# Value and output projection of a shifted-window block: 64-row weights in row tiles replaced by zero-padded 128-row weights in column tiles

## The reference

```python
y = _ln(x, norm1_w, norm1_b); y = jnp.roll(y, (-3, -3), axis=(1, 2))
win = windows(y)                                   # (32 * 64, 49, 64)
q, k, v = split(win @ qkv_w.T)                     # 8 heads of 8
attn = softmax(q @ k^T * scale + bias + mask)      # 49 x 49 for each window and head
out = (attn @ v) @ proj_w.T + proj_b
x = shortcut + roll(out, (3, 3))
z = _ln(x, norm2_w, norm2_b)
return x + gelu(z @ fc1_w.T + fc1_b) @ fc2_w.T + fc2_b
```

## Time and profile before

| what | value |
|---|---|
| median of 3 runs | 2359.13 us (2358.63 to 2376.8) |
| the profiled execution, its own time | 2345.75 us |
| span of its trace | 2343.9 us |
| mean granted TensorE clock | 0.986 |
| PE busy | 2217.1 us, 95% |
| POOL, DVE, ACT busy | 76%, 75%, 66% |

### The profile page before, as it was taken

How to read it: one execution, slowest core, us unless ns; L and a number is a source line. 1 busy time by engine, 2 the same in 40 slices (tenths; PEclk the granted TensorE clock), 3 DMA queues, 4 the chain that set the end, 5 groups by cost and what they waited for, 6 DMA issues and landing times.

```text
span 2343.9 us, 155989 instructions
## 1 busy us (share of the span) xinstructions
PE 2217.1 (95%) x66852; PEld 1699.0 (72%) x66852; DVE 1756.3 (75%) x3230; ACT 1548.0 (66%) x2435; POOL 1770.1 (76%) x1687
## 2 busy tenths in 40 slices
PE   5999999999999999999999999999999999999997
PEld 4777777777777777777777777777677777777775
DVE  5787787777777877777777777777777777777774
ACT  4567666666666776766666766666666666666765
POOL 5787787777777877776777777777777777777774
PEclk7999999999999999999999999999999999999999
DMA  5444444444444454444444444444444444444541
GB/s 122 98 92 103 91 94 100 87 90 90 95 97 90 96 100 90 99 90 85 96 87 92 102 89 93 103 93 90 94 90 89 93 91 97 94 91 93 103 87 41
DMA packets 137659, 217.73 MB, mean 93 GB/s; under 512 B 29336, under 2 KB 95114, under 8 KB 137114
## 3 DMA queue, kind: packets, MB, share of 16 engines
q1 hardware_dynamic: 137114, 208.95, 43.2%
HBM read 131.69 MB, written 77.15 MB: 89 GB/s over the span
## 4 chain that ended last, share of the span: by engine, by line
PE 85%; ACT 6%; issue 5%; DMA 1%; DVE 1%; POOL 0%; SPq 0%; ACTq 0%; POOLq 0%; DVEq 0%
PE O L759 13%; PE ST L745 11%; PE S L723 9%; PE M L767 9%; PE ST L739 8%; PE M L832 7%; PE M L854 7%; PE M L818 5%; PE M L785 5%; PE M L801 5%; PE M L862 3%; ACT L456 3%; ACT gl L456 2%; PE S L727 2%; DMA xin<-in_x 0%
## 5 line engine op out<-in xcount | busy, mean ns | idle before, releaser
L337 POOL TENSOR_TENSOR nmd<-diag,nm 121x392 f16<-121x392 f16 x1024 | 897.4, 885 | 435.6 <-DVE nm L592 412.5
L592 DVE TENSOR_REDUCE nm<-S 121x8 f16<-121x392 f32 x1024 | 576.7, 563 | 375.9 <-PE S L727 185.0
L437 ACT ACTIVATE pT<-ST 113x392 f32<-113x392 f32 x1024 | 506.2, 495 | 404.7 <-PE ST L745 400.2
L759 PEld LDWEIGHTS O<-vx,pT 113*49 113x49 f32 x16384 | 552.1, 127 | 61.1 <-issue 20.5
L759 PE MATMUL O<-vx,pT 113*49 113x18 f32 x16384 | 530.7, 197 | 16.7 <-issue 14.3
L723 PE MATMUL S<-kp,qp 128*49 128x49 f16 x16384 | 395.6, 186 | 26.4 <-issue 10.7
L739 PE MATMUL ST<-qp,kp 128*49 128x49 f16 x16384 | 396.8, 186 | 23.7 <-issue 22.7
L723 PEld LDWEIGHTS S<-kp,qp 128*49 128x49 f16 x16384 | 318.3, 104 | 100.3 <-issue 75.7
L745 PE MATMUL ST<-nmd,shiftw 121*49 121x392 f16 x2048 | 362.6, 350 | 2.0 <-POOL nmd L337 1.3
L739 PEld LDWEIGHTS ST<-qp,kp 128*49 128x49 f16 x16384 | 330.1, 103 | 37.5 <-issue 27.9
L745 PEld LDWEIGHTS ST<-nmd,shiftw 121*49 121x49 f16 x2048 | 107.1, 101 | 286.4 <-issue 150.0
(11 more groups left out here) (87 smaller groups left out, 3297.6 us busy)
## 6 DMA issues: line engine op xcount, KB each, us to landing
parts<-hl SPq DMA_DIRECT2D x512, 98.0 KB, 2.6
qp<-parts SPq DMA_DIRECT2D x512, 98.0 KB
xin<-in_x SPq DMA_DIRECT2D x256, 98.0 KB
kp<-parts SPq DMA_DIRECT2D x256, 98.0 KB
kp<-parts SPq DMA_DIRECT2D x512, 49.0 KB
out<-res SPq DMA_DIRECT2D x256, 98.0 KB
kp<-in_c_keys SPq DMA_DIRECT2D x4, 588.0 KB, 8.4
weights<-in_c_weights SPq DMA_DIRECT2D x1, 384.0 KB, 3.6
```

What stands on the lines that cost most here:

```text
L337: nc.gpsimd.tensor_tensor(nmd[j % LAG][:], diag[:], nm[j % LAG][:].unsqueeze(2).broadcast_to([RM, 2 * 4, N]), ALU.mult).then_inc(s_nmd, 1)
L437: nc.scalar.activation(pT[j % LAG][:].rearrange("k w h q -> k (w h q)"), ST[0:R, j % 2, 0:HK], ACT.Exp).then_inc(s_e, 1)
L592: V.tensor_reduce(nm[j % LAG][:], S[0:RM, 0:HK].rearrange("q (h n) -> q h n", n=N), AX_X, ALU.max, negate=True).then_inc(s_nm, 1)
L759: mm = MM(O[W0 * w:W0 * w + N, (4 * p + hp) * VC:(4 * p + hp + 1) * VC], pT[j % LAG][:, w, hp, :], vx[r % RING][:, window + w, hp, :], sta ...
```

## The change

Both projections are given weights of 128 rows. A host helper `apart` makes them: the 64 x n weights stand twice, once in the upper rows with zeros in the lower ones, once in the lower rows with zeros in the upper ones, side by side in the columns. One matmul over all 128 rows then gives the results of both halves in neighbouring columns.

- `project_v`: 32 matmuls of 64 rows by 49 by 32 columns, in four tiles of the array (two row tiles by two column tiles), two banks, become 16 matmuls of 128 rows by 49 by 64 columns, in two column tiles, one bank.
- `project_out`: 8 matmuls of 64 rows by 113 by 64 columns, in two row tiles, two banks, become 8 matmuls of 128 rows by 49 by 128 columns, in two column tiles, one bank. The halves of the tokens (partitions 0 to 48, 64 to 112) are now separate matmuls.
- The readers (`place_v`, `add_attention`, and `times_v` for the places in `vx`) follow the new places. No wait is added or dropped.
- The weights' load grows from 768 to 896 columns, and DVE also clears all of `M` (128 x 2048) before it computes the tables, since rows 49 to 63 are no longer written by `project_out` and are read by `add_attention`.

```diff
             V.memset(S[:], -1.0).then_inc(c_blank, 1)
             V.memset(ST[:], 0.0).then_inc(c_blank, 1)
             V.memset(O[:], 1.0).then_inc(c_blank, 1)
+            V.memset(M[:], 0.0).then_inc(c_blank, 1)
...
-                    nc.scalar.activation(dst[rows, :, D * e:D * e + D].rearrange("n (a s) d -> n a s d", a=2),
-                                         M[rows, 2:4, 0:256].rearrange("n a (s d) -> n a s d", d=D),
+                    nc.scalar.activation(dst[rows, :, D * e:D * e + D],
+                                         M[rows, 2, :].rearrange("n (s d) -> n s d", d=D),
                                          ACT.Copy).then_inc(s_vx, 1)
...
-                V.tensor_tensor(held, M[0:R, 0:2, 0:4 * C].rearrange("r h (p c) -> r p h c", c=C), held,
+                V.tensor_tensor(held, M[0:R, 0, :].rearrange("r (p h c) -> r p h c", h=2, c=C), held,
                                 ALU.add).then_inc(s_att, 1)
...
             def project_v(u):
                 for s in range(8):
-                    for h in range(2):
-                        for e in range(2):
-                            rows = slice(C * h, C * h + C)
-                            mm = MM(M[W0 * e:W0 * e + N, 2 + h, 32 * s:32 * s + 32], yT[rows, N * s:N * s + N],
-                                    wv[rows, e, :], start=True, stop=True, tile_position=(C * h, W0 * e))
+                    for e in range(2):
+                        mm = MM(M[W0 * e:W0 * e + N, 2, C * s:C * s + C], yT[:, N * s:N * s + N], wv[:, e, :],
+                                start=True, stop=True, tile_position=(0, W0 * e))
                 mm.then_inc(s_vp, 1)
...
                 for q in range(4):
-                    for h in range(2):
-                        rows = slice(C * h, C * h + C)
-                        mm = MM(M[0:R, h, C * q:C * q + C], oT[rows, q, :], wproj[rows, :], start=True, stop=True)
+                    for w in range(2):
+                        mm = MM(M[W0 * w:W0 * w + N, 0, 2 * C * q:2 * C * q + 2 * C], oT[:, q, W0 * w:W0 * w + N], wproj,
+                                start=True, stop=True, tile_position=(0, W0 * w))
                 mm.then_inc(s_pj, 1)
...
+    def apart(a):
+        a = np.asarray(a).reshape(C, -1, a.shape[-1])
+        both = np.zeros((2, C, a.shape[1], 2, a.shape[2]), np.float32)
+        both[0, :, :, 0], both[1, :, :, 1] = a, a
+        return both.reshape(2 * C, -1)
```

More of the change, by code:

```diff
@@ L37 @@
 NVEC = 23 + SPAN
-NWT = 768
+NWT = 896
 RING = 4
@@ L70, in swin_block @@
         wqk = weights[:, 128:256]
[L71 to L74, removed]
+        wproj = weights[:, 256:384]
+        w1 = weights[:, 384:640]
+        wv = weights[:, 640:768].rearrange("c (e f) -> c e f", e=2)
+        w2 = weights[:, 768:896].rearrange("k (a c) -> k a c", a=2)
         st = sb("st", [128, 12, 4])
@@ L193, in swin_block @@
         ZEROED = RING + 2
-        BLANK = 3
+        BLANK = 4
         VALUES = 3 * RING
@@ L755, in times_v @@
                     pe.wait_ge(s_on, 2 * u + j // 4)
-                window = 8 * (j % 2) + 4 * (j // 4) + 2 * ((j % 4) // 2)
+                window = 8 * (j // 4) + 4 * ((j % 4) // 2) + j % 2
                 for hp in range(4):
@@ L759, in times_v @@
                         mm = MM(O[W0 * w:W0 * w + N, (4 * p + hp) * VC:(4 * p + hp + 1) * VC],
-                                pT[j % LAG][:, w, hp, :], vx[r % RING][:, window + w, hp, :],
+                                pT[j % LAG][:, w, hp, :], vx[r % RING][:, window + 2 * w, hp, :],
                                 start=True, stop=True, tile_position=(0, W0 * w))
@@ L972 @@
                every(L0_conv_h_times, L0_conv_ws_scalar, L0_conv_ws_scalar2, L0_conv_pow_para), every(line)]
-    matrices = [ident, twice(qkv[0:2].transpose(3, 0, 2, 1)), twice(np.asarray(L0_conv_proj_w).T),
-                twice(np.asarray(L0_conv_fc1_w).T), twice(qkv[2].reshape(4, 2, D, C).transpose(3, 1, 0, 2)),
+    matrices = [ident, twice(qkv[0:2].transpose(3, 0, 2, 1)), apart(np.asarray(L0_conv_proj_w).T),
+                twice(np.asarray(L0_conv_fc1_w).T),
+                apart(qkv[2].reshape(4, 2, D, C).transpose(3, 1, 0, 2).reshape(C, 2, C // 2)),
                 fc2_wT.reshape(128, 2 * C)]
```

## The result

The changed kernel takes 2259.39 us (median of 4, 2254.02 to 2268.09) against 2358.88 us for the kernel before, a ratio of 0.958 (0.951 to 0.965). The forecast was 2297 us, in a range of 2268 to 2340 us. Its profiled execution took 2254.02 us, 91.7 us less than the profiled one of before.

The account below looks back on a forecast made before the run. PE's stream was taken as the bound. Savings of 17 (output projection), 6 (value projection), 36 (gaps) and 5 (clock), less 2 (start), make 62 us: from the median of 2359 to 2297 us, range 2268 to 2340.

Parts of the forecast that it names:

- The bound and the places: PE's stream bounds the kernel, busy 95% of the span; its instruction gaps come mostly behind the value projection.
- The slower rival: Both projections: weight loads no longer hide behind streams, load and stream take turns; 2421 us, chance 0.04.
- The streams: PE time of the projections: output projection in step 6 saves 17 us, value projection in step 1 saves 6 us.
- DVE's maximum: Step 2, awaited by S: some 0.09 us of slack barely covers step 1's gain of 0.065 us a unit.
- The wait for the first gelu: ACT's chain through table load and gelu to `turn_y` holds PE up by 12.9 us in all and stays so.
- The gaps: PE's waits for instructions, mainly behind the value projection, shrink: 36 us saved, bounds 5 and 59 us.
- The working's three parts: Gap savings: 34 us from value projection to first fc1, 2 us on to second fc1, 1 us in the rest.
- The clock: Long gaps become rarer, so less time at the lower clock level: 5 us saved, bounds 0 and 14.
- The start: DVE's clearing of M stands ahead of the chain through the tables to the first matmul: 2 us lost.
- Theory A: Behind the forecast's gap term: PE runs out of instructions where it passes a packet of 254 fastest, behind the value projection.

Follow-up runs that it names:

- the kernel before with float16: Kernel before, its own projections kept, with the probabilities pT and values vx in float16: 2175.88 us, ratio 0.927.
- spare ones behind the value projection: Changed kernel plus 32 spare float16 matmuls and their 32 loads a unit, right behind the value projection: 2348.53 us, ratio 0.997.
- spare ones behind fc2: Changed kernel plus the same 32 spare matmuls and loads a unit, behind fc2 in step 4: 2346.01 us, ratio 0.998.
- spare ones spread: Changed kernel plus the same 32 spare matmuls and loads a unit, four in each of eight steps behind the scores: 2326.79 us, ratio 0.988.
- changed, float16: Changed kernel with pT and vx in float16 and M cleared in one bank: 2108.37 us, ratio 0.895; run again, 2105.34 us, ratio 0.897.

## Why the prediction was right or wrong

**The bound and the places** were read rightly: PE sets the end, the value projection's own time hardly matters, and the gain comes from the gaps behind it. The weight loads of the two column tiles hide behind the streams: the rounds come every 0.056 and 0.109 us, where load and stream in turn would take 0.099 and 0.153. The slower rival did not come true. The Trainium skill's rule beside it ("TensorE: Matmul & The Clock Gate", section "The mechanism"), that weight loads overlap matmuls in flight only when the row group differs, is not what these rows show for column tiles that share all rows: the measurement decides.

**The streams** were put at 17 + 6 = 23 us and came to 27. Step 6 was sized rightly, and step 1 gave 5 us for 6. The missing 4 us are outside the stretch that was summed: behind each projection O follows the shift 0.015 us sooner. DVE's maximum did cover step 1, as taken: PE waits for it 5 times, 5.4 us, after (3 times, 6.0 us, before). The wait for the first gelu, which was to stay as it is, grew from 12.9 to 18.1 us.

**The gaps** are the step that failed most: 36 us was taken, within bounds of 5 to 59. Measured are 35.7 us of idle time and 56 gaps of 0.16 us less, 45 us. Another 7 us come from delays too short for the count, with under 0.15 us of idle time: against the median of the same place in the unit, they add up to 31 us before and 24 after. So it was 52 us for 36. The mechanism was right, but the working let the number of gaps fall with the length of the stretch (114 matmuls to 82, so 35 of 49 left) and took 0.6 us off each; 13 are left. What counts is from how many places of a unit the next packet's worth passes faster than a packet can be had. With the medians of the unit and 3.4 us (the distance between two packets' starts that 1% fall below), that is 26% of the places before and 2% after. Of the gaps before the second fc1, 17 of 22 went, 6.0 us, where 2 us was taken: a packet that ends there can still have the value projection in it. (The working's three parts, 34 + 2 + 1, also give 37 and not 36.)

**The clock** was taken at 5 us, within 0 to 14. The mean went from 0.986 to 0.993, which halves the time at the lower level, from 66 to 32 us. Behind 70 us it is 36 us before and 6 after, worth at most 15 us; the delays that lie in those stretches outside the gaps went from 10 to 1 us, so 9 to 15 us came for the 5. Before, all seven stretches at the lower level between 70 and 2300 us begin within 1.3 us of the end of a gap of 1.2 to 2.1 us; after, there is one, 1.8 us behind a gap of 1.4 us. So it is the few long gaps that matter here. In other runs the mean does not follow the number of gaps: 40 gaps and 0.987 with the value projection alone, 86 and 0.993 in the kernel before with float16.

**The start** was 2.1 us later, for 2 us taken, but the first fc1 starts at 87.8 us and not 87.3, so the higher clock of the start phase and the shorter stage gave most of it back. On the profiled executions 27 + 52 + 9 to 15 us, less 0.5 for the start and 5 for the gelu, are 83 to 89 of the 91.7 us measured, where 62 was taken: the gaps were short by 16 us, the clock by 4 to 10, the streams by 4. No one of them alone would have left the range. The last 8 us, to the 99 of the medians, are the difference of executions: the profiled execution of before was 13 us faster than the runs' median, the one of after 5 us, and in later runs the kernel before took 2348 to 2354 us, so that the change is worth 91 us there. Against those the gain that was forecast would still be low by about 30 us.

**What the step left out** is shown by the run with the output projection alone: 17 us on PE's path were predicted for that part and 0 came (the interval leaves at most 7); in the profiles the gaps grew by as much. A term was taken as time saved on the bound engine, which it was, but PE was held up by its packets too, and they came no sooner. So the terms of such a sum do not simply add. In the whole change, too, the output projection adds only some 8 us to the value projection's 87 (2259.39 against 2267.06, on different chips). So the projection that was thought to bring 17 us brings some 0 to 8, and the other brings nearly all.

**Theory A** stands, in this form: a gap comes where 127 matmuls pass in less time than a packet needs. The table takes from each profile the time from each matmul's start to the next one's, in the median over the units, and sums 127 of them from every place of a unit.

| kernel | places with under 3.4 us | fastest 127 | gaps for each packet |
|---|---|---|---|
| before | 26% | 2.07 us | 103 / 527 = 0.20 |
| output projection alone | 26% | 2.08 us | 121 / 527 = 0.23 |
| before, float16 | 24% | 2.08 us | 86 / 463 = 0.19 |
| spare ones behind the value projection | 19% | 2.42 us | 96 / 527 = 0.18 |
| spare ones behind fc2 | 6% | 2.57 us | 69 / 527 = 0.13 |
| spare ones spread | 6% | 2.50 us | 67 / 527 = 0.13 |
| changed (and again) | 2% | 2.58 us | 47 / 495 = 0.09 |
| value projection split | 2% | 2.64 us | 48 / 495 = 0.10 |
| value projection alone | 2% | 2.58 us | 40 / 495 = 0.08 |
| changed, float16 (two profiles) | 0% | 3.50 us | 44 and 33 / 431 = 0.10 and 0.08 |
| before, most transfers left out | 26% | 2.10 us | 57 / 527 = 0.11 |

The two places for the spare instructions that were thought to differ are alike by this measure, and so are their gaps. Splitting the value projection could not reduce them, since only 2% was left to take away. Below that some 0.08 to 0.10 gaps a packet stay wherever the instructions stand, and with most other transfers left out nearly all gaps outside the dense stretch go: those come with the traffic. The number of instructions counts through the packets alone, each with its chance of such a gap. The measure was found after the runs and foretold none of them. Why two packets never start less than some 3.3 us apart, with quiet queues too, is not shown by any run here.

## What to carry to other kernels

Where a fully written-out program keeps one engine over 90% busy, divide its instructions by the packets of the instruction queue, and look where in the loop the gaps with "issue" lie. Then take the time in which a packet's worth of instructions passes, from every place of the loop, and compare it with the least distance between two packets (some 3.4 us here). If many places are below it, fewer and longer instructions are worth far more than the time they save themselves, and a shorter stage with as many instructions may be worth nothing. A matmul over 128 rows with half zeros took here about as long as the half-filled tiles did (0.91 us for 0.86 in step 1, 0.89 for 0.94 in step 6), and its group began 0.21 us behind the start of the ST group and not 0.30. Before work is moved to thin out such a stretch, look which neighbour's result is waited for within the next two steps.

## What the runs showed that was not expected

- Time saved on the bound engine can be lost entirely: 20 us in step 6 and behind it gave 0 (ratio 1.000, 0.997 to 1.004), with 18 more gaps in its profile.
- Instructions with next to no work in them, 64 a unit, cost 67 to 89 us, of which 40 to 52 us are their own time.
- With a quarter of the other DMA traffic, about half of the instruction gaps went, and the kernel was 63 us faster.
- All 103 gaps stand at the end of a packet, one place in every 126.8 matmuls.
- The lower clock level follows the longest gaps, of 1.2 to 2.1 us in the kernel before, and not their number.
